# The five issue lists of a two-stream kernel, replaced by five others

## The reference

```
x = x + xattn0(ctx, ln(x)); x = x + rnn(ln(x));     x = x + lora(ln(x))
x = x + xattn1(ln(x), ctx); x = x + linattn(ln(x)); x = x + block1(ln(x))   # causal attention + 4-expert MoE
x = x + xattn2(ctx, ln(x)); x = x + local(ln(x));   x = x + moe2(ln(x))     # 8 experts with capacity
x = x + concat(ln(x), ctx); x = x + ssm(ln(x));     x = x + moe3(ln(x))     # 8 experts, top 1
```

## Time and profile before

| what | value |
|---|---|
| time, median of 3 runs (all) | 2491.32 us (2490.16 to 2494.02) |
| span of the profiled execution | 2495.5 us |
| TensorE busy | 2349.7 us, 94% |
| VectorE, ScalarE, GpSimd busy | 1479.9, 1180.3, 929.6 us |
| TensorE on the chain that ended last | 71% of the span |
| mean granted TensorE clock | 0.989 |
| DMA traffic | 26.57 MB, most of it in the first slice |

### The profile page before, as it was taken

How to read it: one execution, slowest core, us unless ns; L and a number is a source line. 1 busy time by engine, 2 the same in 40 slices (tenths; PEclk the granted TensorE clock), 3 DMA queues, 4 the chain that set the end, 5 groups by cost and what they waited for, 6 DMA issues and landing times.

```text
span 2495.5 us, 41931 instructions
## 1 busy us (share of the span) xinstructions
PE 2349.7 (94%) x16426; PEld 1565.0 (63%) x16426; DVE 1479.9 (59%) x4040; ACT 1180.3 (47%) x2996; POOL 929.6 (37%) x853
## 2 busy tenths in 40 slices
PE   9999989999999999999999999999999999999998
PEld 6665656666766665666666665566566666656665
DVE  5357556665475566666564567665565555664653
ACT  5454334455444534545554444445454444354543
POOL 5235343433233335434231344443322343544410
PEclk9999989999999999999999999999999999999999
DMA  5000000000000000000000000000000000000000
GB/s 233 1 1 1 1 10 9 10 1 18 1 1 10 1 1 10 10 9 9 9 1 9 1 1 9 1 10 9 13 1 1 5 1 1 1 1 1 2 1 9
DMA packets 6821, 26.57 MB, mean 11 GB/s; under 512 B 864, under 2 KB 992, under 8 KB 5984
## 3 DMA queue, kind: packets, MB, share of 16 engines
q1 hardware_dynamic: 6624, 23.89, 2.7%
HBM read 21.79 MB, written 2.10 MB: 10 GB/s over the span
## 4 chain that ended last, share of the span: by engine, by line
PE 71%; DVE 18%; POOL 4%; ACT 4%; issue 3%; DMA 0%; DVEq 0%; POOLq 0%; ACTq 0%
PE ps L486 10%; PE ps L499 6%; PE ps L549 6%; PE ps L518 6%; PE ps L889 4%; PE ps L510 3%; PE ps L628 3%; PE ps L471 3%; PE ps L603 3%; PE ps L596 3%; PE ps L650 3%; PE ps L836 2%; PE ps L601 2%; PE ps L846 2%; PE ps L677 2%
## 5 line engine op out<-in xcount | busy, mean ns | idle before, releaser
L1919 POOL TENSOR_TENSOR P<-P,small 128x384 f32<-128x384 f32 x384 | 317.7, 850 | 555.2 <-DVE small L1430 554.8
L1140 ACT ACTIVATE P<-ps,small 128x192 f32<-128x192 f32 x768 | 314.2, 421 | 147.1 <-DVE small L1422 145.6
L1892 POOL TENSOR_TENSOR small<-small,mhalf 128x4 f32<-128x4 f32 x112 | 128.4, 1147 | 543.4 <-DVE small L1410 272.1
L499 PE MATMUL ps<-kvT,big 128*128 128x192 f32 x1536 | 313.8, 334 | 7.2 <-DVE big L1437 2.8
L499 PEld LDWEIGHTS ps<-kvT,big 128*128 128x128 f32 x1536 | 248.2, 190 | 91.2 <-issue 53.5
L1422 DVE TENSOR_REDUCE small<-ps 128x2 f32<-128x384 f32 x384 | 210.1, 551 | 107.7 <-PE ps L499 100.8
L486 PEld LDWEIGHTS ps<-wts,P 128*128 128x128 f32 x1920 | 231.5, 192 | 43.8 <-issue 30.0
L486 PE MATMUL ps<-wts,P 128*128 128x128 f32 x1920 | 249.0, 279 | 5.2 <-POOL P L2009 2.6
L2009 POOL TENSOR_TENSOR P<-T 128x512 f32<-128x512 f32 x96 | 126.6, 1319 | 206.7 <-ACT T L1289 107.6
L518 PEld LDWEIGHTS ps<-value,big 128*128 128x128 f32 x1536 | 178.1, 192 | 26.9 <-issue 20.7
L518 PE MATMUL ps<-value,big 128*128 128x128 f32 x1536 | 188.4, 277 | 0.5 <-DVE big L1462 0.5
(11 more groups left out here) (288 smaller groups left out, 4483.5 us busy)
## 6 DMA issues: line engine op xcount, KB each, us to landing
ctok<-ctok_dram SPq DMA_DIRECT2D x8, 512.0 KB, 3.7
ctxT<-ctx_dram SPq DMA_DIRECT2D x8, 512.0 KB, 3.9
wts<-weights_dram SPq DMA_DIRECT2D x1, 2530.0 KB, 23.7
wts<-weights_dram SPq DMA_DIRECT2D x1, 2189.0 KB, 18.1
X<-x_dram SPq DMA_DIRECT2D x8, 256.0 KB, 3.0
big<-fold_dram SPq DMA_DIRECT2D x2, 1024.0 KB, 7.9
out_dram<-X SPq DMA_DIRECT2D x8, 256.0 KB, 2.0
wts<-weights_dram SPq DMA_DIRECT2D x1, 1536.0 KB, 26.1
```

The source lines that it names most:

```text
L499: m = pe.matmul(ps[s][:, at:at + KEYS], big[s][:, BANK * b + 128 * p:BANK * b + 128 * p + 128], kvT[s][:, keys_at(b):keys_at(b) + KEYS], s ...
L1140: m = act.activation(probs(s, b // 2)[:, to:to + KEYS], ps[s][:, at:at + KEYS], ACT.Exp, bias=small[s][:, 4 * e + p:4 * e + p + 1], accum_ ...
L1892: pool.tensor_tensor(rstd(s, name, n), variance(s, name, n), mhalf[:, 0:n], ALU.pow).then_inc(*sig("rstd", s))
L1919: m = pool.tensor_tensor(view, view, over(small[s][:, at:at + 2], 2, [128, 2, KEYS]), ALU.mult)
```

## The change

Only the five numbers of `ORDER` change. The counts of segments and of ones in them are the same, so each stream issues the same segments in the same order on each engine, with the same waits, buffers and instructions. What is different is the merging of A and B, on each engine by its own list. The values come from another search. The diff, cut to the first line of each number:

```diff
 ORDER = dict(
     pe=(2498, int(""
-        "404600c8640004010800000000069ebffdf375f56bac10c1af4ddee629cc55cb06914148810afbdc018a1ca1dd3aea84c3e9"
+        "444822181410880258c01020810000335b7b7fb76bb60450b74eddace45a55a981c92142240a7cdd464838a13656dea0b3e9"
...
     act=(1741, int(""
-        "4120206080200000c00039bbffe4faf4fbbecfa82c43130cc0901c000424af78f68bde1856031e6e0e18fee19bfff5810301"
+        "888040194410648209080404e67ff6f67bbef2ab0492a31941100e002110a576bda6f5c23a11356d5141fab51ffffa80826a"
...
     dve=(2030, int(""
-        "1001238a8c0040200000001bbf6bbd7c3b15a5ce31825da73db18614c0dbf16c50d0df8007c68ea4daee65bf0c38303288d8"
+        "10019c448c84102064c044501430ad2f6ecce5e711071e9739cba21341769d70d150b9b21d1c1e314e2edafd8332312308e7"
...
     pool=(610, int(""
-        "6c5018df30532b53182161b93a2fbb7378c7904c253ac34fc0ff53185609d43957dee378c7cb219c0e0dee3a2b53142131b5"
+        "84c56482d685653532821a33934b77e63fb25c04a2531b1afc0ff65229612d4362fbbb1f8db49519a8887db362b52a42162b"
...
     sp=(26, int(""
-        "1333335", 16)))
+        "e0e573", 16)))
```

More of the change, by code:

```diff
@@ L83 @@
-        "ffc1860ae9bffefeffc1f85bf2f38ca502505053d3ced401660e33f2d482affffffffe07ffbdffffeefc192d91eeb2a04181"
-        "2dfb1ff19e1d41389fff30f", 16)),
-    act=(1741, int(""
-        "4120206080200000c00039bbffe4faf4fbbecfa82c43130cc0901c000424af78f68bde1856031e6e0e18fee19bfff5810301"
[L87 to L90, removed]
@@ L91 @@
-    dve=(2030, int(""
-        "1001238a8c0040200000001bbf6bbd7c3b15a5ce31825da73db18614c0dbf16c50d0df8007c68ea4daee65bf0c38303288d8"
[L93 to L97, removed]
+        "444822181410880258c01020810000335b7b7fb76bb60450b74eddace45a55a981c92142240a7cdd464838a13656dea0b3e9"
@@ new lines @@
+        "e32874c2d73bb00200c3ee57fcddffda6c08001268c63565a0105190872de9abc288201348746cb5f6dfebbb0ddc4f3db7fe"
+        "ccd9e70cf2bbfffbfaa87448128a095ef7aa13121a19ed291411ded71eaa4d06b72a42000c5edabfcdbeeaefc1446869d553"
+        "948693bfffc288424a0e4805061000d21b9f9db6f5bdbfedc3fae25fe6df4f5cbcc2556baa8351414884057d866e482c288a"
+        "cf6b4a37bddf7a377f14856cea20080f17ea7e2ded944a0e00cc745b8884324eddffce42d04622000080026badf7eeeb75f4"
+        "85a5b1dde9ffdee5f1e3dad7eff38b448248a058fa73ca13121c38edb4839f4ffffffd67ef77ddffbfff2a38d2db79531010"
@@ new lines @@
+        "15fd17f99eaa89608ea7dff", 16)),
+    act=(1741, int(""
+        "888040194410648209080404e67ff6f67bbef2ab0492a31941100e002110a576bda6f5c23a11356d5141fab51ffffa80826a"
+        "8caaee1010b344a904a00b6e14cfbdf67fffbfed30f173477ffe928f0221182100a972fe2903fe58ac4a0b722548fb2d37ff"
+        "bb860e7bbe2944555f1901e9c0080840d25793f7dffcbfffefbebb20692a561b012016002084466eedd5f75b6e4b5a0db54a"
+        "698f930ffa871a52765b1088acd5b8fe400000201cf6e77becffefbff8cdb35c9d7dd15809026021009a776ce857dffeff7f"
+        "79f7b7dbef0c78df748c95e097de0871ff", 16)),
@@ new lines @@
+    dve=(2030, int(""
+        "10019c448c84102064c044501430ad2f6ecce5e711071e9739cba21341769d70d150b9b21d1c1e314e2edafd8332312308e7"
+        "3466dfaecbbddecf14ca128e5ac0294e48802480148cb6ae89820a5edb6f1f4cfd94675f18f967fff8f03d7e1c3996e71f32"
+        "0b8918eb4630d7e30ea3181192b62ccfebb36e6cb77ffdd60d98e25c9022acc6484a45220000086cdddddddccfa5efe4e5f0"
+        "f3ac6254b8176f26c4950b89c3d1a0f1453b8ddbd99d672f86641d4fb46e6798b7545f7d87131b30988a175cd5404a204008"
+        "183012eddcd9978c8f6a6bff3e78d3b5fd78f137594c655dc2f320b8a196b6b11edefffdf2ffcd7bfff7f1e31c596dbf000e"
+        "b27dfd", 16)),
@@ L98 @@
     pool=(610, int(""
-        "6c5018df30532b53182161b93a2fbb7378c7904c253ac34fc0ff53185609d43957dee378c7cb219c0e0dee3a2b53142131b5"
-        "3af57f8db607c0b9807706bc935fa660ac0ae49ffff3be7d1d", 16)),
+        "84c56482d685653532821a33934b77e63fb25c04a2531b1afc0ff65229612d4362fbbb1f8db49519a8887db362b52a42162b"
+        "936abfef29e2d841784938a97a33fa9512c28e49fffeb67fd1d", 16)),
     sp=(26, int(""
-        "1333335", 16)))
+        "e0e573", 16)))
 def weave(program, order):
```

## The result

| | before | after |
|---|---|---|
| time, median of 4 runs (all) | 2492.67 us (2490.16 to 2500.11) | 2429.68 us (2425.32 to 2432.53) |
| ratio, 95% interval | | 0.9741, 0.9720 to 0.9761 |
| span of the profiled execution | 2495.5 us | 2425.6 us |
| TensorE busy | 2349.7 us | 2312.0 us |
| TensorE idle | 145.8 us | 113.6 us |

A forecast was written before the change was run, and what follows sets the result against it. TensorE was taken as the bound, busy 2349.7 of 2495.5 us, with 145.8 idle. Shorter return-trip shortfalls, 27.2 x 0.73 = 19.9 us, came off the 2491.3 us median: 2471 us, range 2462 to 2484 (8 in 10: 2450 to 2496).

The forecast's parts named there:

- The step that failed: Opening claim: order lists can move only TensorE's 145.8 us of idle time and the stretches at the lower clock.
- Cover was counted in busy time: For 2,070 waiting TensorE segments, listed TensorE work was subtracted from the stream's return trip; shortfalls 145.9 us before, 118.7 after.
- The scale of 0.73: Factor 106.3 / 145.9, from traced waits not held by queues; it turned the raw gain of 27.2 us into 19.9.
- first count: The prediction's sum of return-trip shortfalls on TensorE: 263 short trips, 145.9 us before; 170, 118.7 us after.
- cover in return trips: Other-stream TensorE work listed while a stream goes through other engines and back; claimed as all the change can move, 19.9 us.
- The kinds: Shortfalls by wait: L471 for L1405 41.8 to 54.2 us, L510 for L1919 11.9 to 0.3, L486 for L1502 7.8 to 9.4.
- both named places: B's first `linear` norm: wait from 2.9 to about 1 us; A's first norm of `heads` 2: new wait up to 3.
- TensorE busy within 5 us: Sign of a right forecast: TensorE's busy time stays within 5 us of 2349.7, its idle time near 126 us.
- SP's list at nothing: The list that moves loads by far more than anything else costs nothing, each load having a hundred us or more of cover.
- rival 1: Faster than forecast: raw count of 27.2 us holds and the clock gives 5 more, 2459 us; chance 0.17.
- I take nothing for the middle: Queue holds from ScalarE's, VectorE's and GpSimd's lists: allowance 7 us either way, 20% of 34.7, middle value nothing.
- Rival 3: Slower: instructions held behind the other stream in engine queues, idle time growing by 17 us, to 2508 us; chance 0.17.

The follow-up runs named there:

- experiment 9: Changed kernel with only TensorE's list edited: 149 of 192 attention transposes (L510) one place earlier, before a segment of the other stream; 2488.95 us, ratio 0.9986.
- half of the lists: All five new lists up to a common cut in front of the middle, those of the kernel before behind it; 2463.98 us, ratio 0.9888.
- TensorE's list moved: Kernel before with 522 bits of TensorE's list alone changed by small moves, not parts of the change; 2487.8 us, ratio 0.9979.
- L471 later: Changed kernel with only TensorE's list edited: 149 norm turns (L471) one place later; 2491.37 us, ratio 0.9975.
- searched anew: Changed kernel with TensorE's, ScalarE's, VectorE's and GpSimd's lists searched again using start-to-start spacings; 2423.41 us, ratio 0.9721.
- experiment 8: Changed kernel with the norms' root moved from GpSimd to a VectorE reciprocal, in all norms but `rms` of `moe1`; 2411.25 us, ratio 0.9652.
- experiment 1: The four new engine lists with SyncE's (SP) list of the kernel before; 2430.46 us, ratio 0.9743.
- experiment 4: Kernel before with 476, 476 and 172 bits of ScalarE's, VectorE's and GpSimd's lists changed by small moves, TensorE's list untouched; 2500.9 us, ratio 1.0031.
- experiments 5 and 6: Three extra linked reciprocals ahead of each of the 192 of L1430: in the kernel before 2542.54 us (ratio 1.0191), in the changed kernel 2476.46 us (0.9920).
- experiment 10: Changed kernel with only TensorE's list edited: 140 norm turns (L471) one place earlier; 2593.32 us, ratio 1.0392.

## Why the prediction was wrong

**The step that failed** is in its first paragraph: "what they can move is TensorE's idle time, 2495.5 - 2349.7 = 145.8 us, and the stretches at the lower clock". Busy time held waits too, and the lists moved 37.7 us of it, where at most 5 were allowed. At most 5.8 of these are the clock's, so the second half of the sentence doesn't save it. Two later steps inherit the error:

- *Cover was counted in busy time.* "subtracted the TensorE work listed inside it": that work was valued at what the profile shows as busy, 0.145 us for an L510 before (167.3 / 1152) where unhindered starts lie 0.109 apart. Work that is itself stalled is no cover. With start-to-start spacing for the cover (and ScalarE's accumulator read in the softmax chain, which I had left out) the same count of the same trips gives 196.7 us before and 137.5 after. That is -59.2 us, and the three parts of the measurement that are not the clock sum to -62.3. This count was made after the result, and its nearness is in part luck: the table below has it at half of the measured cost of experiment 9.
- *The scale of 0.73.* It was taken by holding the count against visible idle time, which misses up to 0.2 us at each of 301 waits. It made a count that was too small smaller still: the raw 27.2 us became 19.9, and 32.2 were measured in idle time alone.

How the counts and the replay rank the kernels that differ only in lists (all three made again, so not the numbers of the expectations), as us above the changed kernel (the first count, made again with a later matching of the records, has sums of 149.5 and 119.5 for 145.9 and 118.7; the replay issues the lists with the durations of the trace before and hands a delay on):

| | first count | with spacing | replay | measured |
|---|---|---|---|---|
| before | 30 | 59 | 54 | 65 |
| half of the lists | 17 | 37 | 27 | 37 |
| TensorE's list moved | 27 | 46 | 37 | 59 |
| the other three moved | 30 | 55 | 51 | 72 |
| L510 earlier | 20 | 30 | 47 | 61 |
| L471 earlier | 110 | 104 | 107 | 162 |
| L471 later | 20 | 38 | 67 | 58 |
| searched anew | 3 | -6 | -25 | -5 |

The first count has the sign right in seven of eight rows and the size too small by a factor of 1.5 to 3. The count with spacing is within 6 us for the kernel before, half of the lists and the list searched anew, and 13 to 58 us short in the other five. The replay with the clock's part added (10.5, 60.6 and 2.5 us) gives 57.5, 167.6 and 69.5 for the three hand edits, within 12 us of each. The clock's part was measured and not forecast, so this is a check of the rest and no prediction. For the three lists that came out of a search on such a replay (the two moved and the one searched anew) it is 20 to 22 us too hopeful each time. The replays on record before the runs missed by more: TensorE's moved list was to gain 32 to 37 us and gained 5, and the list searched anew was to gain 33 and gained 5.

**Point by point.**

- The mechanism, cover in return trips, is real and large enough: experiment 9 has the size of the whole change with nothing else edited. How much of the change's own gain is cover on TensorE, and how much the other three lists, no run separates. The kinds were right: norms lose (experiment 8 finds them worth twice as much on the new lists), L471 for L1405 at 38.7 in the forecast 31 to 40, the scan unchanged, both named places (1.75 us for about 1, and 2.75 for up to 3). L510 for L1919 came to 3.6 us, not 2.
- TensorE busy within 5 us: wrong, -37.7 us.
- SP's list at nothing: right (experiment 1). The sign "no TensorE wait on a DMA" failed by one wait of 0.8 us, on a transfer from `fold_dram`, which SyncE issues in the first microseconds and which is no load of that list.
- The clock: -5 us were worked out and stand in rival 1 alone. The -5.8 us of the profiled pair are no confirmation. The four timed executions of the changed kernel lose 23.7 us to the clock on average, those of the kernel before 21 to 26 by session, so no gain is shown.
- "I take nothing for the middle" of the other lists: not tested. Experiment 4 has other lists of these engines at +0.3%, and at B's first `linear` norm a hold in VectorE's queue lengthened the trip by 0.67 us.
- Rival 3, the queues: its sign, waits of L510 for L1167 and L1462 up by 20 us, did not show; they went from 3.6 us to 3.8. The "3 us instruction" L1808 of its reasoning is three instructions (x3 in the earlier trace rows), in the trace before 0.72, 1.20 and 1.20 us; the last two lie beside GpSimd's L1919. Rival 1 was the nearest; its clock gain is not shown, and it was itself 30 us short.

**What stays open.** Why experiments 5 and 6 cost 45 to 48 us each, when the counts said 62 and 35, was not found, nor why experiment 9 costs twice what the count with spacing gives. Nor was it shown what makes searched lists miss by 20 us. How VectorE's instructions stretch in a new order (described below) is in no count and is a candidate; that was only argued.

## What to carry to other kernels

Before counting how much an order can gain on TensorE, measure its stalls from start to start, against the spacing inside an unhindered run of the same line. Idle time under-read them here by 0.16 to 0.2 us for each wait, and busy time of stalled work is not cover. Where waits grow, read the granted clock of the stretches behind them and add its price (experiment 10), and compare profiled executions only together with their clocks. Judge a searched order by a run: all three here came out 20 us or more above their replay.

## What the runs showed of the hardware

**VectorE beside GpSimd.** In the fence at 329 us, `rescale` on VectorE starts 0.06 us after GpSimd's L372 of 1.90 us and takes 2.39 us. The same instruction in a quieter place of the changed kernel, and once more in a busy one:

```profile
1012.20 0.68 DVE L1405 TENSOR_TENSOR P<-X,small 128x512 f32<-128x512 f32 x1
...
1118.63 2.48 DVE L1405 TENSOR_TENSOR P<-X,small 128x512 f32<-128x512 f32 x1
```

In the trace before, the 50 executions of L1405 without any GpSimd instruction beside them have a median of 692 ns. The 33 that have one beside them for nine tenths of their time or more have 1094 ns, and one in ten of them takes some 2478 ns. VectorE instructions that read PSUM (L1422 at 557 ns, L1454 and L1462 at 691) show no such stretch.

The length follows a sum. Twenty-three executions in the two traces started behind one single GpSimd instruction of 384 columns or more (L372, L1919, L1929, L2004, L2009) that had 0.5 us or more still to run. Each took what that instruction had left and 0.545 to 0.549 us more: 1.84 + 0.55 = 2.39 at 329.06. Two kinds of neighbour do nothing. Beside L1892 or L1989, GpSimd instructions of 4 columns that last 1.0 us or more, L1405 took 682 to 694 ns in all 25 cases. And in the four cases in which L1405 started first it took 684 to 691 ns.

The Trainium skill ("SBUF — State Buffer", section "Who interferes with whom") says that a VectorE instruction with two SBUF inputs contends with a GpSimd instruction that reads SBUF, that the port pair which they share is an exclusive lock, and that the order of issue decides who is blocked. By that rule, the trace agrees for the wide neighbours. For the narrow ones it shows no block to the end of the instruction, though they read SBUF too.

So part of what looks like a long norm is a neighbour on GpSimd, and an order of VectorE's and GpSimd's lists that keeps the two apart could gain there. That wasn't tried.
